# Turning normalised rows for a feed-forward layer by VectorE blocks and a DRAM round trip instead of TensorE transposes

## The reference

```python
x = layernorm(x + attention(x, Wq, bq, Wk, bk, Wv, bv, Wo, bo))      # rotary positions, softmax
g = einsum('th,ih->ti', x, gate_w) * gate_s
u = einsum('th,ih->ti', x, up_w) * up_s                              # ternary weights: -1, 0, 1
x = layernorm(x + einsum('ti,hi->th', silu(g) * u, down_w) * down_s)
```

## Time and profile before

| | |
|---|---|
| median of 3 runs | 1087.38 us (1084.76 to 1093.31) |
| the profiled execution | 1084.82 us, its span 1082.9 us |
| granted TensorE clock over the span | 0.998 |

### The profile page before, as it was taken

How to read it: one execution, slowest core, us unless ns; L and a number is a source line. 1 busy time by engine, 2 the same in 40 slices (tenths; PEclk the granted TensorE clock), 3 DMA queues, 4 the chain that set the end, 5 groups by cost and what they waited for, 6 DMA issues and landing times.

```text
span 1082.9 us, 15122 instructions
## 1 busy us (share of the span) xinstructions
PE 1039.6 (96%) x5788; PEld 556.5 (51%) x5788; DVE 789.0 (73%) x900; ACT 649.2 (60%) x1224; POOL 263.7 (24%) x226
## 2 busy tenths in 40 slices
PE   8999999999999999999999999999999999999996
PEld 3643344433443433443444433333337888888885
DVE  5789978899779799779888899999703465463544
ACT  2358876788678788678666688888753431222221
POOL 1651030041335522245210043644000000000002
PEclk9999999999999999999999999999999999999999
DMA  6074416243242512444140447521207110010011
GB/s 235 39 192 124 104 36 208 51 95 85 53 111 74 95 62 46 89 96 104 33 76 18 108 129 163 152 63 33 109 10 207 68 40 1 1 38 2 1 39 41
DMA packets 36732, 87.49 MB, mean 81 GB/s; under 512 B 12528, under 2 KB 12912, under 8 KB 34448
## 3 DMA queue, kind: packets, MB, share of 16 engines
q1 hardware_dynamic: 36080, 85.76, 30.0%
q10 hardware_dynamic: 576, 0.72, 0.2%
HBM read 49.76 MB, written 23.86 MB: 68 GB/s over the span
## 4 chain that ended last, share of the span: by engine, by line
PE 53%; ACT 7%; DVE 2%; DMA 1%; issue 1%; SPq 0%; POOL 0%; POOLq 0%
PE PSA L1178 14%; PE PV L590 13%; PE PS L570 12%; ACT Bn L576 6%; PE PS L1225 5%; PE PS L713 2%; PE PSA L713 2%; PE PV L1225 1%; PE PS L278 1%; ACT Bn L606 1%; DVE nmx L509 1%; DMA wr<-A 1%; PE PSA L498 1%; PE PSA L1123 1%; DVE x1a L716 0%
## 5 line engine op out<-in xcount | busy, mean ns | idle before, releaser
L509 DVE TENSOR_REDUCE nmx<-PSA 128x1 f32<-128x1024 f32 x512 | 599.6, 1216 | 88.0 <-PE PSA L498 87.9
L576 ACT ACTIVATE Bn<-PS 128x512 f32<-128x512 f32 x1024 | 528.9, 605 | 147.4 <-PE PS L570 146.7
L570 PE MATMUL PS<-Qt,Kt 50*128 50x512 f32 x1024 | 373.4, 446 | 27.0 <-ACT Bn L576 14.0
L498 PE MATMUL PSA<-Kt,Qt 48*128 48x512 f32 x1024 | 394.3, 463 | 2.1 <-DVE nmx L509 1.0
L570 PEld LDWEIGHTS PS<-Qt,Kt 50*128 50x128 f32 x1024 | 167.3, 184 | 322.5 <-ACT Bn L576 299.5
L590 PE MATMUL PV<-Bn 128*32 128x512 f32 x2048 | 272.8, 605 | 0.0
L498 PEld LDWEIGHTS PSA<-Kt,Qt 48*128 48x128 f32 x1024 | 166.4, 184 | 30.2 <-DVE nmx L509 13.8
L1178 PE MATMUL PSA<-x1Th,wr 128*128 128x512 f32 x344 | 136.2, 396 | 1.0 <-DMA wr<-A 0.5
L1178 PE MATMUL PSA<-x1Tl,wr 128*128 128x512 f32 x344 | 134.4, 391 | 0.0
L1198 DVE SCALAR_TENSOR_TENSOR sg<-PSA,us,sg 128x512 f32<-128x512 f32 x43 | 32.1, 748 | 115.1 <-ACT sg L1189 114.8
L1189 ACT ACTIVATE sg<-PSA,gs 128x512 f32<-128x512 f32 x43 | 29.5, 689 | 138.2 <-PE PSA L1178 138.2
(11 more groups left out here) (161 smaller groups left out, 834.0 us busy)
## 6 DMA issues: line engine op xcount, KB each, us to landing
Qt<-pscr SPq DMA_DIRECT2D x90, 128.0 KB, 4.9
A<-in_wf SPq DMA_DIRECT2D x11, 768.0 KB, 6.2
wr<-A SPq DMA_DIRECT2D x33, 256.0 KB, 2.7
pscr<-A SPq DMA_DIRECT2D x16, 512.0 KB, 3.7
vscr<-Bn SPq DMA_DIRECT2D x32, 256.0 KB, 2.0
Kt<-pscr SPq DMA_DIRECT2D x90, 64.0 KB, 2.4
A<-in_xT SPq DMA_DIRECT2D x4, 1024.0 KB, 7.7
A<-A SPq DMA_DIRECT2D x16, 256.0 KB, 3.7
```

The lines of the kernel that those rows point to most:

```text
L498: r = pe.do(lambda e, h=h, p=p: e.matmul(ps[:, h, :], Qt[i][p:p + NC_, g % 2, 128 * qt:128 * qt + 128], Kt[i][p:p + NC_, 512 * h:512 * h + ...
L509: r_mxs[hh, s] = dve.do(lambda e: e.tensor_reduce(nmx[:, hh % 2, c0:c0 + 1], ps, AX.XY, ALU.max, negate=True), c_rel[s])
L570: r = pe.do(lambda e: e.matmul(PS2[:, c % 3, :], Kt[i][rows, 128 * kt:128 * kt + 128], Qt[i][rows, g % 2, 512 * qh:512 * qh + 512], start= ...
L576: r_exp[c] = act.do(lambda e: e.activation(Pb[c % NP_], PS2[:, c % 3, :], ACT.Exp, scale=0.25), c_exp)
```

## The change

The rows are no longer transposed by TensorE in the exact branch. VectorE turns each 32x32 block of 256 rows (`turn_blocks`: two instructions on 128x512), one DMA writes the result to a DRAM buffer `tscr`, and four DMAs per block `tb` (`read_x1`) read it back so that whole rows come out turned: each takes 32 partitions x 4 x 16 runs of 32 floats (128 bytes), 2048 runs, 256 KB. `split_x1` then makes high and low parts from SBUF. The waits of the turned rows are placed by hand: the DMAs of tb 0 at unit 241 and its splits after units 245 and 246; for tb 1 the reads at pass 3, the splits at 5 and 6; for tb 2 at 16, and 18 and 19; for tb 3 at 22, and 26 and 27. The projections of batch 1 move from passes 16 and 17 to 14 and 15, and the splits of the output weights from 12 to 15 to two each at 12 and 13.

```diff
+        c_tb = count("c_tb")
+        c_ty = [count(f"c_ty{i}") for i in range(4)]
+        r_ty = {}
+
+        def turn_blocks(b, t2, y, *waits):
+
+            tb, pair = 2 * b + t2 // 2, t2 % 2
+            dve.wait(r_x1[b, t2], *waits)
+            for j in range(2):
+                r = dve.do(lambda e, j=j: e.transpose(y[:, 512 * j:512 * j + 512], x1[b][:, 2 * t2 + j, :]), c_tb)
+            sp.wait(r)
+            out = tscr[tb, 256 * pair:256 * pair + 256, :].rearrange("(j p) c -> p j c", p=128)
+            r_ty[tb, pair] = sp.do(lambda e: e.dma_start(out, y.rearrange("p (j c) -> p j c", j=2)), c_ty[tb], 16)
...
+            if i >= 6:
+                sp.wait(r_ty[0, 0], r_ty[0, 1], r_ty[1, 0])
...
+        def norm_and_turn(t2):
+            whole(outs[t2])
+            turn_blocks(0, t2, A[:, 9216 + 1024 * t2:10240 + 1024 * t2], r_parts[1, 3])
+
         for t2 in range(4):
             spread(outs[t2], 10 + t2 // 2, 3 + 8 * (t2 % 2), ())
         for t2, (n, w) in enumerate(((10, 11), (11, 3), (11, 11))):
-            before[n, w] = lambda t2=t2: whole(outs[t2])
+            before[n, w] = lambda t2=t2: norm_and_turn(t2)
...
+        def read_x1(tb, *waits):
+
+            sp.wait(r_ty[tb, 0], r_ty[tb, 1], *waits)
+            stage = x1Tx[tb % 2][1]
+            src = tscr[tb].rearrange("(a i) (k b j) -> b i k a j", i=32, b=4, j=32)
+            for g in range(4):
+                dst = stage[32 * g:32 * g + 32, :, :].bitcast(F32).rearrange("p k (a j) -> p k a j", j=32)
+                r_tx[tb] = sp.do(lambda e, g=g, dst=dst: e.dma_start(dst, src[g]), c_tx[tb], 16)
+
+        put(15, 1, lambda: read_x1(0, r_s2last[NG - 2]))
...
+            def split_x1(tb, *ks):
+
+                hi, lo = x1Tx[tb % 2]
+                for k in ks:
+                    src = lo[:, k, :].bitcast(F32)
+                    q, c = (dve, c_xl) if tb == 0 else (act, c_xt)
+                    q.wait(r_tx[tb])
+                    if tb == 0:
+                        r = q.do(lambda e, k=k, src=src: e.tensor_copy(hi[:, k, :], src), c)
+                    else:
+                        r = q.do(lambda e, k=k, src=src: e.copy(hi[:, k, :], src), c)
+                    dve.wait(r, r_tx[tb])
+                    r = dve.do(lambda e, k=k, src=src: e.tensor_tensor(
+                        lo[:, k, :], src, hi[:, k, :].bitcast(F32), ALU.subtract), c_xl)
+                    r_xt[tb] = r_xt.get(tb, []) + [r]
...
-                if exact and tb >= 1:
-                    waits = [r_wr[i, p] for i in range(1, 5) for p in range(2)] if tb == 1 else [r_gu[tb - 2]]
-                    act.wait(*waits)
-                    dve.wait(*waits)
...
-                    if exact:
-                        hi, lo = (x[:, :, c0:c0 + 128] for x in x1Tx[tb % 2])
-                        if tb == 0:
-                            dve.wait(r_fill)
-                            r = dve.do(lambda e, hi=hi, src=src: e.tensor_copy(hi, src), c_xl)
-                        else:
-                            r = act.do(lambda e, hi=hi, src=src: e.copy(hi, src), c_xt)
-                        dve.wait(r, r_fill)
-                        r = dve.do(lambda e, hi=hi, lo=lo, src=src: e.tensor_tensor(
-                            lo, src, hi.bitcast(F32), ALU.subtract), c_xl if j == 0 else c_rel[s])
...
-                act.wait(r_late["wo"], r_at[7], *(r_wr[4, p] for p in range(2)))
+                act.wait(r_late["wo"], r_at[7], r_ty[1, 1], *(r_wr[4, p] for p in range(2)))
...
-            pieces = {q: lambda f=f, k=k: f(k) for q, (f, k) in zip(
-                (7, 8, 9, 10, 12, 13, 14, 15), [(f, k) for f in (split_rows, split_out) for k in range(KT)])}
+            pieces = {q: [] for q in range(4 * FI)}
+            for q, f in ((2, lambda: turn_blocks(0, 3, A[:, 6160:7184], r_wr[4, 0], r_wr[4, 1])),
+                         (3, lambda: read_x1(1, *(r_wr[i, p] for i in range(1, 5) for p in range(2)))),
+                         (5, lambda: split_x1(1, 0, 1)), (6, lambda: split_x1(1, 2, 3)),
+                         *((7 + k, lambda k=k: split_rows(k)) for k in range(KT)),
+                         *((12 + k // 2, lambda k=k: split_out(k)) for k in range(KT)),
+                         *((16 + t2 // 2, lambda t2=t2: turn_blocks(1, t2, (
+                             *(wo[:, 2 * j:2 * j + 2, :].rearrange("p j c -> p (j c)") for j in range(2)),
+                             A[:, 14848:15872], A[:, 15872:16896])[t2], r_pj[1])) for t2 in range(4)),
+                         (16, lambda: read_x1(2, r_gu[0])),
+                         (18, lambda: split_x1(2, 0, 1)), (19, lambda: split_x1(2, 2, 3)),
+                         (22, lambda: read_x1(3, r_gu[1])),
+                         (26, lambda: split_x1(3, 0, 1)), (27, lambda: split_x1(3, 2, 3))):
+                pieces[q].append(f)
...
-                if exact and u in (U - 12, U - 11):
-                    turn_x1(0, u - U + 12)
+                if exact and u in (U - 11, U - 10):
+                    split_x1(0, *range(2 * (u - U + 11), 2 * (u - U + 11) + 2))
...
-            OP = FI + 5 if exact else 3
-            turns_at = (8, 9) if exact else (4, 6)
+            OP = FI + 3 if exact else 3
+            turns_at = (4, 6)
...
-                if exact and q in pieces:
-                    pieces[q]()
-                if i in turns_at and tb < 3:
+                if exact and q < 4 * FI:
+                    for f in pieces[q]:
+                        f()
+                if not exact and i in turns_at and tb < 3:
                     turn_x1(tb + 1, turns_at.index(i))
```

More of the change, by code:

```diff
@@ L77, in post_ln_layer @@
     vscr = nc.dram_tensor("vscr", [8, 256, 1024], F32, kind="Internal").ap()
+    tscr = nc.dram_tensor("tscr", [4, 512, 512], F32, kind="Internal").ap()
     rscr = nc.dram_tensor("rscr", [8, 8, 1024], F32, kind="Internal").ap()
@@ L1045, in unit @@
                     f()
+        x1Tx = [[at(f"x1T{p}{n}", o + 8192 * j, [128, KT, 512], F32R) for j, p in enumerate("hl")]
+                for n, o in enumerate((12288, 32 * ((base_a + 8223) // 32) - base))]
+        c_tx = [count(f"c_tx{i}") for i in range(4)]
+        r_tx = {}
+        def read_x1(tb, *waits):
[6 more added lines that the diff above has]
+        put(15, 1, lambda: read_x1(0, r_s2last[NG - 2]))
         for u in range(SPLIT):
@@ L1072, in post_ln_layer @@
         hTx = [[at(f"hT{p}{i}", 2048 * (2 * i + j), [128, 512], F32R) for j, p in enumerate("hl")] for i in range(2)]
-        x1Tx = [[at(f"x1T{p}{n}", o + 8192 * j, [128, KT, 512], F32R) for j, p in enumerate("hl")]
-                for n, o in enumerate((12288, 32 * ((base_a + 8223) // 32) - base))]
         KEPT = 6
@@ L1126, in turn_x1 @@
                                   c_fill if (j, k) == (1, KT - 1) else None)
-                r_fill = r
-                if tb > 0 or not exact:
-                    act.wait(r, r_s2last[NG - 2])
-                if exact:
-                    dve.wait(r_s2last[NG - 2])
-                if exact and tb >= 1:
-                    waits = [r_wr[i, p] for i in range(1, 5) for p in range(2)] if tb == 1 else [r_gu[tb - 2]]
-                    act.wait(*waits)
-                    dve.wait(*waits)
[L1136 to L1139, removed]
+                act.wait(r, r_s2last[NG - 2], r_tx[0], *free_b)
+                if tb >= 2:
+                    act.wait(r_gu[tb - 2])
                 for j in range(2):
@@ L1142, in turn_x1 @@
                     src = ps[:, j, :].rearrange("p (k c) -> p k c", k=KT)
-                    if exact:
-                        hi, lo = (x[:, :, c0:c0 + 128] for x in x1Tx[tb % 2])
-                        if tb == 0:
-                            dve.wait(r_fill)
-                            r = dve.do(lambda e, hi=hi, src=src: e.tensor_copy(hi, src), c_xl)
-                        else:
-                            r = act.do(lambda e, hi=hi, src=src: e.copy(hi, src), c_xt)
-                        dve.wait(r, r_fill)
-                        r = dve.do(lambda e, hi=hi, lo=lo, src=src: e.tensor_tensor(
-                            lo, src, hi.bitcast(F32), ALU.subtract), c_xl if j == 0 else c_rel[s])
-                    else:
-                        r = act.do(lambda e, c0=c0, src=src: e.copy(x1Tf[tb % 2][:, :, c0:c0 + 128], src),
-                                   c_xt if j == 0 else c_rel[s])
+                    r = act.do(lambda e, c0=c0, src=src: e.copy(x1Tf[tb % 2][:, :, c0:c0 + 128], src),
+                               c_xt if j == 0 else c_rel[s])
                 r_xt[tb] = r_xt.get(tb, []) + [r]
```

## The result

The changed kernel takes **1104.7 us** (median of 4 runs, 1102.8 to 1106.9) against 1086.07 for the kernel before, measured beside it: ratio 1.016 [1.011, 1.021]: slower by about 1.6%. The profiled execution took 1105.5 us (span 1103.7, granted clock 0.986), 20.7 more than that of before.

What follows compares the result with a forecast made beforehand. TensorE, busy for 1039.6 of 1082.9 us, was taken as nearly the only bound in the passes. The terms, -3.0 + 19.2 + 5.9 + 0.6 + 2 = +24.7 us on the profiled 1084.8, gave 1109.5, said as 1110 us; range 1092 to 1142.

Steps and rivals of the forecast that it cites:

- Removed transposes, -7.6: Attention and passes: 64 TensorE transposes in eight groups go, giving back 2.1 us and 5.5 us, 7.6 in all.
- VectorE's turns, +2.8: Attention: three pairs of turns, 1.3 us each, delay the additions that free TensorE's banks; +2.8 us, bounds 0 and 3.9.
- Projections two passes earlier, +1.3: Behind pass 13: TensorE reaches the output weights' last split before VectorE has finished it; +1.3 us, bounds 0 and 3.
- Pass 2, +0.5: VectorE waits for tile 4's last weights' copy and turns 1.3 us before multiplying for pass 3; +0.5 us, bounds 0 and 2.
- L = 14 us: Time from the first of a block's four read issues to the last landing, 12 us of it packets.
- the first rival: Read-backs: the engines take small packets back to back, 8.5 us from first issue to last landing; 1096 us, chance 0.18.
- Block 1, L + 5.2: After gate_up of pass 7: TensorE stands still for reads whose write queues behind all copies; +19.2 us.
- Block 2, L - 8.1: After gate_up of pass 20: TensorE stands still because the reads block from pass 18; +5.9 us.
- Block 0, +0.6: End of attention: reads go out at about 762.3 and their split rows are needed at unit 248; +0.6 us.
- The clock, +2: After long stalls matmuls may begin at 1.2 GHz; +2 us, between nothing and 5.4 for each stall.
- how long a read-back takes: The step sizing read-backs of 8192 small runs: between 8.5 and 23 us, 14 taken through a geometric middle for packets.
- The third rival: Block 1's reads are not late, so no stall: 1082 us, or 1077 with the turns hidden too; chance 0.10.

Runs made afterwards that it cites:

- e4: The changed kernel without VectorE's three pairs of turns in attention, those rows written unturned: 1107.11 us, ratio 1.014 [1.006, 1.022].
- e1: The changed kernel with block 1's splits after passes 8 and 9 in place of 5 and 6: 1086.79 us, ratio 1.0003.
- e7: The changed kernel with block 1's write and reads issued ahead of the last nine weights' copies, splits unmoved: 1099.91 us, ratio 1.013.
- e5: The changed kernel with block 1's splits after passes 8 and 9, block 2's after 19 and 20, two output-weight splits at pass 10: 1087.87 us, ratio 1.0001.
- e8: The kernel of e6 with block 1's splits at passes 9 and 10, two output-weight splits at pass 8: 1083.2 us, ratio 0.998.
- e2: The changed kernel with read-backs in runs of 2 KB in place of 128 bytes, rows not turned: 1099.36 us, ratio 1.012.
- e3: The changed kernel with eight unused TensorE transposes put back after each of units 244 and 245: 1108.37 us, ratio 1.016.
- e6: The kernel of e5 with block 0 transposed by TensorE, no turns in attention, both block 1 turns in pass 2: 1084.12 us, ratio 0.999.
- e9: The kernel of e5 with eight unused TensorE transposes after each of units 244 and 245: 1085.56 us, ratio 0.998.
- e10: The kernel of e8 with all four block 1 splits in pass 9 and two attention splits moved to passes 10 and 11: 1083.77 us, ratio 0.9985.

## Why the prediction came out so

The forecast was 1109.5 us and the profiled execution took 1105.5. The sum was 24.7, the loss 20.7, and part of the nearness is luck: two errors of opposite sign. Term by term:

- *Removed transposes, -7.6.* Held: 3.64 became 2.61 us, 6.35 became 5.44.
- *VectorE's turns, +2.8.* A pair took 1.31 us, as the upper end had it; the cost was 3.4 us by position and 3.7 by e4.
- *Projections two passes earlier, +1.3.* TensorE waited 1.1 us for the last output-weight split.
- *Pass 2, +0.5.* Held. VectorE stood 3.3 us for tile 4's copy and turned from 832.46 on, and TensorE waited 0.3 us at 835.95 for the low part of pass 3. By position the kernel was 7.0 us behind at 793.03 and 7.5 at the end of `gate_up` of pass 7 (852.6 against 845.1). Not tested by itself.
- *L = 14 us.* This is the mis-sized term: 10.3 in block 1, 9.4 in block 2 (951.23 to 960.66), between the short end of 8.5 and the forecast. DMA of the changed kernel, 852 to 864 us, in slices of 0.3 us:

```profile
DMA  2000001999999999999999999999999700000000
```

The packets of the four reads flowed from 854.0 to 861.7. These are 7.7 us for 512 packets an engine, 15 ns each, with the engines full: back to back, as the first rival said, and near the 12.7 ns of the earlier trace rows, not at the pace of that row, which would have made 21 us. The forecast's 12 us of packets was a middle between these two readings, and the step that failed is the weight that it gave to the gaps in the row. The share of the DMA engines does not give a packet's cost: it is 1.65 from 856 to 860, more than 16 engines can be busy, so it adds up packets whose times overlap. The pace was not even, 1354 and 1437 packets in the first two microseconds and 949 to 1073 in each of the next five; why is open. The Trainium skill's rule ("DMA: Bandwidth & Descriptors", "Why small descriptors are slow (HBM only)") would have had 4.8 us for the packets; the trace has 7.7, so the beat overhead alone does not explain them.

- *Block 1, L + 5.2.* The form held. With 10.3 it gives 15.5, and TensorE waited 14.5. The 1.0 between them is that the write landed (849.06 + 3.50 = 852.56) just as `gate_up` of pass 7 ended and not 1.0 us behind it. e1 and e7 confirm both of its halves.
- *Block 2, L - 8.1.* With 9.4 it gives 1.3; 0.3 us was waited, against the +5.9 of the sum. *Block 0, +0.6:* TensorE did not wait. Here the long L did the damage to the sum: 4.7 + 5.6 + 0.6 = 11 us too much.
- *The clock, +2.* The part that was foreseen, matmuls at 1.2 GHz behind the stall, measures 1.97 + 0.36 = 2.3 us. The part that was not foreseen is the fall near 779: the kernel should have left that stretch 3.4 - 2.1 = 1.3 us behind and left it 7.0 behind: 5.7 us, in the profiled execution.

Added up from the trace: -7.6 + 3.4 + 1.1 + 0.5 + 14.5 + 0.3 + 2.3 + 5.7 = +20.2, against 20.7. The mechanism, one stall behind `gate_up` of pass 7 that the queues hand on, was right. The step that failed is "how long a read-back takes", and the clock step was blind to a fall without a stall. With L = 10.3 the prediction's own sum would have been -3.0 + 15.5 + 2.2 + 0 + 2 = +16.7, as far under the measured loss as the forecast was over it. The third rival (reads not late) was an accurate price list: e1 shows that with the stall taken away the kernel stands at 1.0003 [0.997, 1.003] of before. Its further promise of -3.0 us is not seen there; the three kernels with block 0 on TensorE come near it by their medians, but not clear of no change, and -7.6 was never seen.

## To carry to other kernels

Replacing work of a busy engine by a DMA round trip gains only the work, 7.6 us here, and risks the whole landing: before asking how long the transfer is, find in the queue of the issuing engine what stands ahead of it, and in the queues of its consumers what stands behind them. Place the consumers where they can wait (three passes later: 17 of the 18.6 us between the medians), and again look which engine is full in that pass. When two such kernels are compared by less than 1%, list each execution's mean clock beside its time, since one profile may hold a fall of the clock that another execution lacks.

## What was not expected of the hardware

The clock of TensorE falls without a stall, in some executions. In the profiles it fell between 775 and 785 us in the changed kernel, e1, e4, e5 and e8, and not in before, e2, e3, e6, e7, e9 and e10. TensorE was busy for 3.1 of the 4 us in the row 776 to 780 of the changed kernel and of e8. The program of e7 is the same as the changed kernel's up to there, and so is its work, but its clock stayed up (the same columns):

```profile
776.00:780.00 4.00, 3.10 (x18) 0.97 (x21) 3.72 (x8) 3.46 (x7) 0.00 (x0) 1.00 0.46 172
```

So what TensorE does there does not alone decide on the fall. e5's profile has one more fall (clock 0.50 from 70 to 74 us, where before has 1.00), far ahead of everything that the change touches. The Trainium skill ("TensorE: Matmul & The Clock Gate", "Part 1: The HAM clock gate (the "warmup" mystery)") has the clock set by how busy TensorE has been of late, and its lower level belong to an idle one; the trace has it fall with the engine at work in each unit. A mean clock at or below 0.991 was seen in 11 of 85 executions of before, 8 of 36 of the kernels with block 0 on TensorE (e6, e8, e10), 8 of 20 of e1 and e5, and 2 of 12 of e9. Whether the removed transposes make the fall more frequent is open: the counts lean that way, e8 shows that transposes don't rule it out, a mean clock does not tell where it fell, and 12 executions are too few.

The issue of a DMA of 2048 runs keeps SP's queue for 1.38 us (median), against 0.43 for the same 256 KB in runs of 2 KB (e2). This is 5.6 us of queue time for four reads, in which nothing behind them is issued.
